# Second matrix product of a gated feed-forward block on one Trainium2 core: two of four hidden blocks as three float32r products

## The chip, the cores and the metric

The kernel runs on one core of one Trainium2 chip (trn2). The metric is the device time of one execution in microseconds, and lower is better. The engines are named as the profile names them: PE is TensorE, DVE is VectorE, ACT is ScalarE, POOL is GpSimd, and SP is the queue that issues most DMAs.

## The reference, cut to what matters

The input is 32 images of 128 channels and 56 x 56 pixels. A convolution of signs with batch norm is added to the input (phase 1 of the kernel, and the relu at the head of phase 2). Then each pixel is a token of 128 values, and the feed-forward part below is computed. Weights are float32, and so is the result.

```
weights = x @ wr + br                              # router, one number per token
sel     = the top k - 1 tokens of an image, k = 1568
h       = gelu(sel @ w1 + b1)                      # 128 -> 512
y       = (h @ w2 + b2) * weights[selected]        # 512 -> 128, the product that is changed
out     = scatter of y into zeros, + x
```

The kernel computes h and y for all tokens and multiplies y by a gate, which is zero for tokens that are not chosen.

## The kernel before, in words

An image is a [128 channels, 3136 tokens] tile, cut into 7 chunks of 448 tokens. Phase 1 (the first 500 us) centres the channels, takes signs, convolves and gathers the batch statistics. Phase 2 does everything else, image by image, and is the part that the change touches.

Phase 2 is a schedule that is written by hand. Every engine walks through the same 56 positions for an image (`POS`), 8 for a chunk, and does at each position what tables assign to it. At positions 0 to 3 of a chunk PE computes one hidden block each (`hidden`, three float16 products of 128x448 into one bank), and ACT applies the gelu and writes `hs` (L495, float32, a ring of two chunks with four blocks). At positions 4 to 7 PE multiplies the hidden blocks 0 to 3 of the chunk before by `w2_c` in float32 and sums them in one bank (`output`, L950). A block is so used 12 positions after it was computed, and ACT takes the sum after the fourth (L505).

The other work of phase 2 is put between these by the tables, in positions of an image. Those of interest here:

- `TRANSPOSE_AT`: PE transposes a chunk of the next image into one of two banks (L885), and DVE takes statistics of it (L647). The first four are at 1, 3, 4 and 5, the rest at 9, 10 and 11.
- Position 14: DVE turns the statistics into variances (L660 to L665). Position 15: POOL takes their power -0.5 (L426). Position 22: DVE `mean_over_std` (L670). Position 23: PE transposes mean and deviation (L904), DVE splits them in three (L676 to L679), and SP spreads them into rows by DMA. PE needs the rows at position 31 (L917).
- `NORM_AT`: PE spreads the statistics over the channels (L917, L920), DVE scales (L685) and centres (L694) the tokens, ACT and POOL write the high half `th` (L518) and the low half `tl` (L412), and DVE writes `base` (L702).
- `ROUTER_AT`: PE computes the router's products (L895), the last at position 27. DVE writes the row at 28 (L709), SP stores it and loads it back in another layout, and only then issues the load of the second half of the next `x` and `y`, which ACT waits for at position 37 (L511).
- `COUNT_AT`, eight rounds at positions 35, 39, 42, 46, 50, 53, 58 and 61 (58 and 61 are 2 and 5 of the next image): PE sums counts (L959), DVE chooses a threshold (L728, L733, L739) and counts again (L722). A round can't begin before the one before it has come back.
- Positions 66 to 69 (10 to 13): DVE and PE rank the ties, and DVE writes the gates (L767 to L775). SP spreads them by DMA, and PE needs them at position 19 (L930). DVE multiplies y by them (L781), and POOL adds `base` (L419).

Each engine takes its instructions in order, so one that waits holds back all that follow on its engine. The lines of the change are in `output` (PE), a new `hidden_high` on DVE and a new `hidden_low` on POOL.

## Time and profile before

| what | value |
|---|---|
| three runs | 2378.2, 2380.06, 2380.43 us; median 2380.06 |
| the profiled execution | 2379.78 us, its span 2377.8 us |
| PE, DVE, ACT, POOL busy in the span | 93%, 68%, 51%, 39% |
| mean granted clock of TensorE | 0.981 |
| from one power operation on POOL (one in each image) to the next, mean of 31 | 56.0 us, from 531.6 to 2267.8 us |

The page gives busy time of each engine for the whole span. Since the work of phase 2 repeats with the image, the more useful reading is one image in order of time: what each engine does at a position, and what it waits for there. The images alternate between some 58 and 55 us.

### The profile page before, as it was taken

How to read it: one execution, taken by the hardware profiler on the slowest of the kernel's cores; microseconds unless marked ns; L12 is line 12 of the kernel's file. 1: busy time of each engine (PE TensorE's matmuls, PEld its weight loads, DVE VectorE, ACT ScalarE, POOL GpSimd, SP SyncE). 2: the span in 40 equal slices, each digit the busy share in tenths (PEclk: the TensorE clock that was granted, in tenths of full speed). 3: DMA queues.
4: the chain of work that ended last, by engine and by line, in shares of the span. 5: the costliest groups of instructions: out<-in, count | busy, mean ns of one | idle time of the engine just before them, and what ended most of it. 6: DMA issues, size and time to landing. Idle time of an engine off the chain costs nothing. (4 is left out here: it accounts for less than half of the span.)

```text
span 2377.8 us, 38759 instructions
## 1 busy us (share of the span) xinstructions
PE 2202.0 (93%) x9739; PEld 1071.6 (45%) x9739; DVE 1622.5 (68%) x4887; ACT 1222.9 (51%) x2030; POOL 918.5 (39%) x714
## 2 busy tenths in 40 slices
PE   6999999966999999999999999998999999999997
PEld 3555555533444444444444444444444444444443
DVE  6777777755677766767676666666667676767764
ACT  4444444434555555555555555555555555555553
POOL 1000000024455544445445555454544454554433
PEclk9999999987999999999999999999999999999998
DMA  3444444431122222222222222222222222222201
GB/s 146 163 162 162 162 162 162 162 122 46 62 73 73 74 81 76 81 85 75 73 73 73 73 73 72 73 73 73 81 82 91 73 73 73 73 73 84 73 33 59
DMA packets 66710, 216.99 MB, mean 91 GB/s; under 512 B 28496, under 2 KB 33328, under 8 KB 62640
## 3 DMA queue, kind: packets, MB, share of 16 engines
q1 hardware_dynamic: 66464, 215.71, 25.1%
q14 instruction: 84, 0.69, 0.1%
q8 instruction: 18, 0.29, 0.1%
q10 hardware_dynamic: 144, 0.30, 0.0%
HBM read 136.70 MB, written 77.47 MB: 90 GB/s over the span
## 5 line engine op out<-in xcount | busy, mean ns | idle before, releaser
L950 PE MATMUL ps<-hs,w_c 128*128 128x448 f32 x1792 | 806.9, 564 | 0.8 <-ACT yo L505 0.6
L495 ACT ACTIVATE hs<-ps,b1c,undo 128x448 f32<-128x448 f32 x896 | 602.6, 718 | 136.6 <-PE ps L941 136.0
L412 POOL TENSOR_TENSOR tl<-tr,th 128x448 f16<-128x448 f32 x224 | 245.5, 1096 | 515.7 <-ACT th L518 393.9
L854 PE MATMUL ps<-yo,cwT 128*128 128x448 bf16 x2016 | 425.6, 356 | 0.0
L950 PEld LDWEIGHTS ps<-hs,w_c 128*128 128x128 f32 x1792 | 305.3, 192 | 191.7 <-issue 152.3
L505 ACT ACTIVATE yo<-ps,cols 128x448 f32<-128x448 f32 x224 | 141.9, 633 | 453.6 <-PE ps L950 453.6
L407 POOL TENSOR_TENSOR xb<-xb,zr 128x448 f32<-128x448 f32 x224 | 259.1, 1159 | 182.7 <-ACT zr L511 181.8
L419 POOL TENSOR_TENSOR yo<-yo,base 128x448 f32<-128x448 f32 x224 | 264.5, 1181 | 167.4 <-DVE yo L781 166.6
L939 PE MATMUL ps<-th,w_h 128*128 128x448 f16 x896 | 321.4, 359 | 0.0
L941 PE MATMUL ps<-th,w_l 128*128 128x448 f16 x896 | 319.3, 356 | 0.0
L940 PE MATMUL ps<-tl,w_h 128*128 128x448 f16 x896 | 319.2, 356 | 0.0
L854 PEld LDWEIGHTS ps<-yo,cwT 128*128 128x128 bf16 x2016 | 179.2, 98 | 196.2 <-issue 48.7
L476 ACT ACTIVATE y<-ps 128x448 f16<-128x448 f32 x224 | 121.9, 544 | 263.2 <-PE ps L854 263.2
L781 DVE TENSOR_TENSOR yo<-yo,ps 128x448 f32<-128x448 f32 x224 | 138.6, 619 | 152.4 <-PE ps L930 150.7
L647 DVE BATCH_NORM_STATS2 st<-ps 112x6 f32<-112x128 f32 x896 | 192.7, 282 | 62.9 <-PE ps L885 60.5
L511 ACT ACTIVATE zr<-y,bn_t,bn_s 128x448 f32<-128x448 f16 x224 | 168.8, 754 | 122.2 <-DMA y<-y_int 109.6
L685 DVE TENSOR_TENSOR ur<-xb,ps 128x448 f32<-128x448 f32 x224 | 138.5, 618 | 134.8 <-PE ps L917 76.5
L571 DVE BATCH_NORM_STATS2 base<-y 128x448 f16 (+1 forms) x224 | 140.5, 627 | 130.2 <-ACT y L476 130.2
L518 ACT ACTIVATE th<-tr 128x448 f16<-128x448 f32 x224 | 129.3, 577 | 139.8 <-DVE tr L694 127.6
L426 POOL TENSOR_TENSOR rm<-stw,kt 112x28 f32<-112x28 f32 x32 | 153.6, 4799 | 78.8 <-DVE stw L665 78.8
L885 PE MATMUL ps<-kt,xb 128*112 128x128 f32 x896 | 140.4, 281 | 41.7 <-DVE st L647 28.8
L403 POOL TENSOR_TENSOR sm<-sm,kt 128x1 f32<-128x1 f32 x1 | 0.6, 566 | 459.7 <-DVE sm L635 459.7
(131 smaller groups left out, 2709.7 us busy)
## 6 DMA issues: line engine op xcount, KB each, us to landing
xb<-x SPq DMA_DIRECT2D x31, 1568.0 KB, 7.6
xb<-x SPq DMA_DIRECT2D x33, 896.0 KB, 4.7
result<-yo SPq DMA_DIRECT2D x32, 896.0 KB, 4.4
y_int<-y SPq DMA_DIRECT2D x32, 784.0 KB, 3.7
xb<-x SPq DMA_DIRECT2D x33, 672.0 KB, 4.3
result<-yo SPq DMA_DIRECT2D x32, 672.0 KB, 3.4
y<-y_int SPq DMA_DIRECT2D x32, 448.0 KB, 5.3
y<-y_int SPq DMA_DIRECT2D x32, 336.0 KB, 4.8
```

The costliest lines, as they stand in the source:

```text
L407: nc.gpsimd.tensor_tensor(cut(xb[b], c), cut(xb[b], c), zr[(b + c) % 2][:, :], ALU.add).then_inc(x1_ready, 1)
L412: nc.gpsimd.tensor_tensor(cut(tl, c), tr[(b + c) % 2][:, :], cut(th, c), ALU.subtract).then_inc(tl_ready, 1)
L419: nc.gpsimd.tensor_tensor(cut(yo[b], c), cut(yo[b], c), cut(base[b], c), ALU.add).then_inc(out_ready, 1)
L426: nc.gpsimd.tensor_tensor(rm[:, 0, :], stw[:, 5, :], kt[0:TILE, K_MHALF:K_END], ALU.pow).then_inc(rstd_ready, 1)
L495: nc.scalar.activation(hs[(b + slot) % 2][:, j, :], ps[:, H_BANK + j, 0:T], ACT.Gelu_apprx_tanh, bias=b1c[:, j:j + 1], scale=undo[:, 1:2]) ...
L511: nc.scalar.activation(zr[(mb + c) % 2][:, :], cut(y16[mb], c), ACT.Relu, bias=bn_t[:, :], scale=bn_s[:, :]).then_inc(relu_ready, 1)
L647: last = V.bn_stats(st[:, c * TPG + i, :], ps[0:TILE, BC0 + c % 2, i * C:(i + 1) * C])
L854: last = M(bank, cwT[:, t, :], sg[b][:, c * ROWS + dy:c * ROWS + dy + ROWS, dx:dx + SIDE], start=t == 0, stop=t == TAPS - 1)
L939: M(bank, w1_h[:, blk], cut(th, c), start=True, stop=False)
L940: M(bank, w1_h[:, blk], cut(tl, c), start=False, stop=False)
L941: M(bank, w1_l[:, blk], cut(th, c), start=False, stop=True).then_inc(h_done, 1)
L950: last = M(bank, w2_c[:, j, :], hs[(b + c) % 2][:, j, :], start=first, stop=final)
```

## The change

Hidden blocks 0 and 1 of each chunk are no longer multiplied in float32. DVE casts `hs` to float32r (`hh`), POOL writes the rest `hl = hs - hh`, also float32r, and PE forms three float32r products for each block: `w2_h` x `hh`, `w2_h` x `hl`, `w2_l` x `hh`. The weights are split once, in phase 1. Blocks 2 and 3 stay as they were. The casts stand at positions 1 and 2 of a chunk on DVE, the subtractions at 2 and 3 on POOL.

```diff
+SPLIT = 2
...
+        w2_h = sb("w2_h", [C, SPLIT, C], f32r)
+        w2_l = sb("w2_l", [C, SPLIT, C], f32r)
...
+        hh = [sb(f"hh{b}", [C, SPLIT, T], f32r) for b in range(2)]
+        hl = [sb(f"hl{b}", [C, SPLIT, T], f32r) for b in range(2)]
...
+            def hidden_low(n, b, c, j):
+                pool.wait_ge(hh_ready, (n * NCH + c) * SPLIT + j + 1)
+                ring = (b + c) % 2
+                nc.gpsimd.tensor_tensor(hl[ring][:, j, :], hs[ring][:, j, :], hh[ring][:, j, :].bitcast(f32),
+                                        ALU.subtract).then_inc(hl_ready, 1)
...
+                    slot, j = divmod(pos, 2 * NB)
+                    if 2 <= j < 2 + SPLIT and has(n):
+                        hidden_low(n, b, slot, j - 2)
...
+            link(V.tensor_copy(w2_h[:, :, :], w2_c[:, 0:SPLIT, :]))
+            V.tensor_tensor(w2_l[:, :, :], w2_c[:, 0:SPLIT, :], w2_h[:, :, :].bitcast(f32), ALU.subtract)
...
+            def hidden_high(n, b, c, j):
+                dve.wait_ge(h_ready, (n * NCH + c) * NB + j + 1)
+                ring = (b + c) % 2
+                V.tensor_copy(hh[ring][:, j, :], hs[ring][:, j, :]).then_inc(hh_ready, 1)
...
+                    if 1 <= j < 1 + SPLIT and has(n):
+                        hidden_high(n, b, slot, j - 1)
...
-                last = M(bank, w2_c[:, j, :], hs[(b + c) % 2][:, j, :], start=first, stop=final)
+                ring = (b + c) % 2
+                if j < SPLIT:
+                    pe.wait_ge(hl_ready, g * SPLIT + j + 1)
+                    M(bank, w2_h[:, j, :], hh[ring][:, j, :], start=first, stop=False)
+                    M(bank, w2_h[:, j, :], hl[ring][:, j, :], start=False, stop=False)
+                    M(bank, w2_l[:, j, :], hh[ring][:, j, :], start=False, stop=False)
+                else:
+                    last = M(bank, w2_c[:, j, :], hs[ring][:, j, :], start=False, stop=final)
```

Three places show where the new instructions stand. The first is DVE between positions 23 and 34 of an image, from the end of the split of the statistics to the first count. Before:

```order
L702 SCALAR_TENSOR_TENSOR base<-tr,xb 128x448
L781 TENSOR_TENSOR yo<-yo,ps 128x448
L709 TENSOR_SCALAR wrow<-ps,undo,cols 7x448
L781 TENSOR_TENSOR yo<-yo,ps 128x448
L685 TENSOR_TENSOR ur<-xb,ps 128x448
L694 TENSOR_TENSOR tr<-ur,ps 128x448
L781 TENSOR_TENSOR yo<-yo,ps 128x448
L722 TENSOR_SCALAR junk,cnt_c<-wse,cand 128x392
```

And now (line numbers of the changed kernel; `hh<-hs` is the new cast):

```order
L720 SCALAR_TENSOR_TENSOR base<-tr,xb 128x448
L799 TENSOR_TENSOR yo<-yo,ps 128x448
L804 CAST hh<-hs 128x448 x2
L727 TENSOR_SCALAR wrow<-ps,undo,cols 7x448
L799 TENSOR_TENSOR yo<-yo,ps 128x448
L703 TENSOR_TENSOR ur<-xb,ps 128x448
L712 TENSOR_TENSOR tr<-ur,ps 128x448
L799 TENSOR_TENSOR yo<-yo,ps 128x448
L804 CAST hh<-hs 128x448
L740 TENSOR_SCALAR junk,cnt_c<-wse,cand 128x392
```

Two casts have come in ahead of the router's row, and one ahead of the first count.

The second is DVE at positions 40 to 45, between two rounds of the search. Before:

```order
L694 TENSOR_TENSOR tr<-ur,ps 128x448
L728 TENSOR_SCALAR reached,srch<-ps 128x15
L733 TENSOR_SCALAR srch<-srch,steps 128x1
L739 TENSOR_SCALAR srch<-srch,candc 128x1
L702 SCALAR_TENSOR_TENSOR base<-tr,xb 128x448
L722 TENSOR_SCALAR junk,cnt_c<-wse,srch 128x392
```

And now:

```order
L712 TENSOR_TENSOR tr<-ur,ps 128x448
L804 CAST hh<-hs 128x448
L746 TENSOR_SCALAR reached,srch<-ps 128x15
L751 TENSOR_SCALAR srch<-srch,steps 128x1
L757 TENSOR_SCALAR srch<-srch,candc 128x1
L804 CAST hh<-hs 128x448
L720 SCALAR_TENSOR_TENSOR base<-tr,xb 128x448
L740 TENSOR_SCALAR junk,cnt_c<-wse,srch 128x392
```

One cast stands ahead of the choice and one ahead of the next count. The rounds at 50 and 58 have the same pair around them.

The third is POOL from position 15 to 24. Before:

```order
L426 TENSOR_TENSOR rm<-stw,kt 112x28
L412 TENSOR_TENSOR tl<-tr,th 128x448
L407 TENSOR_TENSOR xb<-xb,zr 128x448
L419 TENSOR_TENSOR yo<-yo,base 128x448
L412 TENSOR_TENSOR tl<-tr,th 128x448
L407 TENSOR_TENSOR xb<-xb,zr 128x448
```

And now (`hl<-hs,hh` is the new subtraction):

```order
L439 TENSOR_TENSOR rm<-stw,kt 112x28
L419 TENSOR_TENSOR tl<-tr,th 128x448
L425 TENSOR_TENSOR hl<-hs,hh 128x448
L414 TENSOR_TENSOR xb<-xb,zr 128x448
L425 TENSOR_TENSOR hl<-hs,hh 128x448
L432 TENSOR_TENSOR yo<-yo,base 128x448
L419 TENSOR_TENSOR tl<-tr,th 128x448
L414 TENSOR_TENSOR xb<-xb,zr 128x448
```

Two subtractions have come in ahead of the second `tl`, which the router's last product needs.

## Rows read from the trace of the kernel before

**Rows 1.** The page: busy time of the engines, and two of its costliest groups.
```profile
PE 2202.0 (93%) x9739; PEld 1071.6 (45%) x9739; DVE 1622.5 (68%) x4887; ACT 1222.9 (51%) x2030; POOL 918.5 (39%) x714
...
L950 PE MATMUL ps<-hs,w_c 128*128 128x448 f32 x1792 | 806.9, 564 | 0.8 <-ACT yo L505 0.6
...
L511 ACT ACTIVATE zr<-y,bn_t,bn_s 128x448 f32<-128x448 f16 x224 | 168.8, 754 | 122.2 <-DMA y<-y_int 109.6
```

**Rows 2.** Busy time by stretch (length, engines, clock, DMA share, GB/s): an image, two parts.
```profile
1020.57:1078.37 57.80, 53.05 (x230) 24.88 (x228) 39.18 (x131) 31.04 (x50) 28.70 (x22) 1.00 0.21 75
...
1099.20:1124.50 25.30, 24.41 (x101) 11.37 (x101) 20.62 (x76) 13.16 (x22) 10.99 (x10) 1.00 0.32 124
1066.50:1078.40 11.90, 11.79 (x60) 6.51 (x61) 10.22 (x48) 5.86 (x10) 3.80 (x4) 1.00 0.29 109
```

**Rows 3.** Timeline of PE (start, length, engine, line, tiles): prices of products.
```profile
252.58 0.53 PE L844 MATMUL ps<-xh,centre_r 128*128 128x448 f32 x1
252.95 0.37 PE L845 MATMUL ps<-xl,centre_r 128*128 128x448 f32 x1
...
254.73 0.53 PE L844 MATMUL ps<-xh,centre_r 128*128 128x448 f32 x1
...
1089.78 0.35 PE L895 MATMUL ps<-th,wsel_h 128*128 128x448 f16 x1
1089.97 0.35 PE L895 MATMUL ps<-tl,wsel_h 128*128 128x448 f16 x1
...
1100.00 2.49 PE L950 MATMUL ps<-hs,w_c 128*128 128x448 f32 x6
1102.43 0.36 PE L930 MATMUL ps<-rows,ones_b 3*128 3x448 bf16 x1
```

**Rows 4.** Groups by line over the whole span: the cast nearest to the new one.
```profile
L547 DVE CAST xh<-xb 128x448 fp32r<-128x448 f32 x224 | 84.7, 378 | 7.2 <-PE ps L845 6.8 <-DVE cand L622 0.4
```

**Rows 5.** Timeline, POOL and DVE, 1078 to 1088 us: both engines on SBUF at once.
```profile
1078.37 4.80 POOL L426 TENSOR_TENSOR rm<-stw,kt 112x28 f32<-112x28 f32 x1 [2.48 <-DVE stw L665]
...
1084.13 1.14 POOL L407 TENSOR_TENSOR xb<-xb,zr 128x448 f32<-128x448 f32 x1
...
1086.31 1.04 POOL L412 TENSOR_TENSOR tl<-tr,th 128x448 f16<-128x448 f32 x1
...
1079.62 0.63 DVE L702 SCALAR_TENSOR_TENSOR base<-tr,xb 128x448 f32<-128x448 f32 x1
...
1084.72 0.59 DVE L670 SCALAR_TENSOR_TENSOR rm<-stw,rm 112x28 f32<-112x28 f32 x1
```

**Rows 6.** Timeline, 1105 to 1123 us: ACT, PE and DVE between rounds of the search.
```profile
1105.48 0.76 ACT L511 ACTIVATE zr<-y,bn_t,bn_s 128x448 f32<-128x448 f16 x1 [5.97 <-DMA y<-y_int]
...
1107.32 0.71 ACT L495 ACTIVATE hs<-ps,b1c,undo 128x448 f32<-128x448 f32 x1
...
1109.66 0.17 PE L959 MATMUL ps<-cand_sel,cnt_c 128*128 128x15 f16 x1
...
1122.64 0.62 PE L885 MATMUL ps<-kt,xb 128*112 128x128 f32 x4
...
1106.24 0.17 DVE L728 TENSOR_SCALAR_CACHE_REDUCE reached<-ps 128x15 f32<-128x15 f32 x1
...
1107.86 0.61 DVE L722 TENSOR_SCALAR_CACHE_REDUCE junk<-wse,srch 128x392 bf16<-128x392 f32 x1
```

**Rows 7.** Timeline, 1075 to 1100 us: PE and DVE where a DMA or a round ends a wait.
```profile
1081.34 0.34 PE L930 MATMUL ps<-rows,ones_b 3*128 3x448 bf16 x1 [0.28 <-DMA rows<-mks]
...
1095.11 0.36 PE L917 MATMUL ps<-rows,ones_b 3*128 3x448 bf16 x1 [1.10 <-DMA rows<-rms]
...
1099.90 0.18 PE L959 MATMUL ps<-cand_sel,cnt_c 128*128 128x15 f16 x1 [1.21 <-DVE junk L722]
...
1075.02 0.25 DVE L767 TENSOR_SCALAR mk<-ps,srch 98x32 f32<-98x32 f32 x1 [0.90 <-PE ps L972]
...
1090.55 0.73 DVE L709 TENSOR_SCALAR wrow<-ps,undo,cols 7x448 f32<-7x448 f32 x1 [0.50 <-PE ps L895]
```

More of the change, by code:

```diff
@@ L251, in block_kernel @@
         h_ready = sem("h_ready")
+        hh_ready = sem("hh_ready")
+        hl_ready = sem("hl_ready")
         y_done = sem("y_done")
@@ L781, in apply_gate @@
                 V.tensor_tensor(cut(yo[b], c), cut(yo[b], c), ps[:, BC1, 0:T], ALU.mult).then_inc(gated, 1)
+            def hidden_high(n, b, c, j):
+                dve.wait_ge(h_ready, (n * NCH + c) * NB + j + 1)
+                ring = (b + c) % 2
+                V.tensor_copy(hh[ring][:, j, :], hs[ring][:, j, :]).then_inc(hh_ready, 1)
             def phase2(n, b):
                 for pos in range(POS):
+                    slot, j = divmod(pos, 2 * NB)
                     at = (n, b, pos)
```

## The prediction

> **What bounds the kernel now.** I read the page first, then the busy time of single images and stretches, then the timelines of the engines in one image. The page [rows 1] shows PE busy for 93% of the span, with the float32 product L950 as its largest group, and DVE at 68%. That alone says: make PE cheaper. It doesn't say where PE's time can be taken away. In one image [rows 2] PE is busy for 53.05 of 57.80 us, DVE for 39.18, ACT for 31.04 and POOL for 28.70. But DVE's load is uneven. In the stretch of the search (positions 35 to 61) DVE is busy for 20.62 of 25.30 us, and in the next one, up to the variance, for 10.22 of 11.90. Its free time lies elsewhere, mostly between positions 19 and 35.
>
> PE has short waits where something else ends last [rows 7]: 0.28 us for the gates' rows (position 19), 1.10 us for the rows of statistics (position 31), and 1.21 us for the first count (position 35). All three are ends of chains that start on DVE or pass it. What is put on DVE ahead of them comes out on PE in full.
>
> **PE's price.** Three float32 blocks in a row take from 1100.00 to 1102.43 us, 0.81 us each [rows 3]. Float16 products start 0.19 us apart. In phase 1 a group of nine bfloat16 and two float32r products repeats every 2.15 us (252.58 to 254.73); less 9 x 0.19 that leaves 0.44, or 0.22 for a float32r product. Three of them make 0.66, so a block gains 0.15 us. The ends: 0.19 each (as float16) gives 0.57 and a gain of 0.24; 0.37 each (the distance from the first float32r product to the second, with the weight load in it) gives 1.11 and a loss of 0.30. I take 0.15, since the period counts both and everything around them. An image has 14 such blocks. Two (positions 28, 29) lie before the wait at 31, whose end is set by a DMA: worth nothing. The other 12 would give 1.8 us an image.
>
> **DVE's price.** The cast has a twin in phase 1, 0.378 us [rows 4], with POOL idle. Here POOL works. When both use SBUF they wait for each other: L670, with 28 elements a row, takes 0.59 us and ends at 1085.31, just after POOL's L407 has ended at 1085.27 [rows 5]. So a cast may wait for up to one whole POOL operation, 1.14 us, and at least for nothing. I take 0.5, about half of one: the first cast releases POOL's subtraction of the same block, and the second comes while that runs. A cast then costs 0.88 us, between 0.38 and 1.52.
>
> The Trainium skill (SBUF — State Buffer, engine side) says that VectorE in a two-port mode or with two SBUF inputs and GpSimd take a shared port pair as an exclusive lock for the whole instruction. It speaks against this change. L670 and L407 agree; the long power operation doesn't, see the rivals.
>
> **The sum, for one image.**
> 1. *Search, positions 35 to 61.* Six casts (41, 42, 49, 50, 57, 58) add 5.3 us to DVE's 20.62, which makes 25.9 in a stretch of 25.30: +0.6. PE's own saving there (eight blocks, 1.2 us) isn't seen, for DVE ends last. To this comes a new wait. The cast at 41 needs `hs` of position 40, and ACT has that only after the relu at 37, which waited 5.97 us for a DMA [rows 6]: ACT starts the gelu at 1107.32 and ends at 1108.03, while DVE had come to its choice at 1106.24. That is 1.8 us of waiting, with the choice, the candidate and the next count (1107.86) queued behind, and PE waits for that count at 1109.66. ACT's wait for that DMA is 109.6 us over 30 cases on the page's group (3.7 us on average, estimated from its total), so I take half of the 1.8: +0.9. Together +1.5 us. Bounds: -1.2 (all hidden, PE's saving whole) and +3.
> 2. *To the gates and the variance, positions 5 to 14.* Two casts (9, 10) add 1.8 us to 10.22 in 11.90 us. DVE's own wait of 0.90 us before the gates (1075.02) takes some of it, and the rest delays the gates, hence the DMA, hence PE at position 19, which waits for it already: +1.0. Bounds: 0 and +1.8. POOL's power operation begins that much later too, and so do the statistics.
> 3. *19 to 23.* Two blocks (20, 21) at 0.15: -0.3. Bounds -0.5 and +0.6. The casts at 17 and 18 fall into DVE's idle time; without it they would cost 0.8.
> 4. *23 to 35.* Two casts (25, 26) come between the statistics' split and the router's row, 1.8 us against DVE's wait of 0.50 us there (1090.55). The row's store and reload carry that to the first count, for which PE waits: +1.2. Bounds: 0 and +1.8. The casts at 33 and 34 come ahead of or with the wait for that reload: nothing, or 0.4 if it lands early.
>
> POOL gets 14 subtractions of about 1.14 us, 16 us an image on top of 28.70 in 57.80: 78% busy, not a bound on average. It is tightest behind the power operation. The `tl` that the router's last product needs ended at 1087.35 [rows 5] and moves by two subtractions to 1089.6; PE starts that product at 1089.78 [rows 3]. I cost it at nothing; if those 0.2 us are gone it is some 0.5 us an image. The products themselves come 10 positions after their subtraction, with POOL's lag well inside. Splitting the weights in phase 1 is two short operations in DVE's gaps: nothing.
>
> The sum is 1.5 + 1.0 - 0.3 + 1.2 = **+3.4 us an image**, with 32 images 109 us. Against the profiled execution of 2379.78 us (0.3 us below the median of the runs) that is **2488 us**, 4.6% slower. What a measurement of this kernel can tell from no change is about 0.2%, or 5 us.
>
> **The rivals.**
> - *PE's saving comes through.* DVE idles for 18.6 us an image, and 14 casts need 5.3 without port waits. If the port waits are short and ACT is early, casts slip into gaps and PE pays nothing. For it: PE is 93% busy, and most of DVE's idle time is waiting for PE. Against it: the two stretches where DVE is at 82% and 86%, and the search, in which DVE must answer PE each round. All of it gives 12 x 0.15 x 32 = 58 us, 2322; half of it 2351. It decides where DVE's additions in the search stay below its idle 4.7 us there with PE's 1.2 taken off, that is below 3.5 us or 0.58 a cast. Chance 0.22.
> - *Gains and waits cancel* within 5 us: 0.04.
> - *Every wait is met in full.* Items at their upper ends, 3 + 1.8 - 0.3 + 1.8 = 6.3 us an image: 2581. For it: casts and subtractions release each other, so collisions are systematic. Against it: delays of one chain partly cover those of the next. Chance 0.12.
> - *The power operation locks the casts out.* POOL's L426 takes 4.80 us in each image, and the casts at 17 and 18 come while it runs. Waiting for its end would delay the gate multiplication at 19 and PE behind it by some 2 us, 64 in all: 2552. Against it: a two-input operation of DVE ran inside it in 0.63 us, its usual time (1079.62) [rows 5]. Chance 0.03. This is what the Trainium skill's rule on that page (a lock held for the full instruction) would give when taken by the letter; the trace doesn't agree for this operation.
> - *The float32r triple isn't cheaper on PE.* At 0.37 us a product, 14 blocks lose 0.30 each: 134 us on PE alone, so 2514 even if nothing waits. The second float32r product of phase 1 came without such a delay. Chance 0.03.
>
> **How the numbers follow.** The forecast, slower through DVE, has 0.56; its own range is 2410 to 2560 (about +1 to +5.6 us an image). Slower in all: 0.56 + 0.12 + 0.03 + 0.03 = 0.74; same 0.04; faster 0.22. The range of 8 in 10 takes in the upper part of the faster cases and stops short of the full ones: 2330 to 2570.
>
> **What would show it.** In the changed profile L950's group must have half its records, and the triple must repeat every 0.6 to 0.7 us. If I am right, PE's busy time falls by some 50 to 70 us while its waits for DVE's count (L959) and for DMA rows grow by more; DVE shows casts with a mean well above 0.38 us and a spread up to 1.5; the time from one power operation to the next rises from 56.0 to about 59.4 us. It is wrong if casts take 0.38 to 0.45 us on average, if PE's waits for counts stay at about a microsecond an image, or if that period falls below 56.

## The result and the profile after

The changed kernel takes 2678.74 us (median of four runs, the lowest 2675.14), the kernel before in the same session 2380.00: a ratio of 1.1252, 95% interval [1.123, 1.1274], so 299 us slower. One of the four executions was in a slower state (2733.80 us); the ratio is of the other three. The forecast was slower by 109 us, to 2488. The direction was right, the size was not, and 2678.74 lies above the range of 2330 to 2570.

The page of the changed kernel: the busy times that answer to [rows 1], and groups by line (busy time, mean ns of one, idle time before, releaser).

```profile
PE 2268.8 (85%) x10187; PEld 1181.0 (44%) x10187; DVE 2059.6 (77%) x5337; ACT 1222.3 (46%) x2030; POOL 1480.1 (55%) x1162
...
L983 PE MATMUL ps<-hs,w_c 128*128 128x448 f32 x896 | 456.7, 619 | 0.0
...
L804 DVE CAST hh<-hs 128x448 fp32r<-128x448 f32 x448 | 289.6, 651 | 35.7 <-ACT hs L511 35.1
...
L720 DVE SCALAR_TENSOR_TENSOR base<-tr,xb 128x448 f32<-128x448 f32 x224 | 221.3, 988 | 0.1
```

The float32 group has half its records, as it must. But PE's busy time rose by 67 us instead of falling by 50 to 70. A float32 record now lasts 619 ns on average, where it lasted 564 [rows 1]. Sorted by the granted clock, the records at full clock are as before (567 ns, 560 before), and those at the lower level take 995 ns: there are 86 of these now, of 896, where there were 12 of 1792. So the mean rose because the granted clock fell. The casts' mean is 0.65 us. `base`, an old operation, rose from 735 ns (its group before the change) to 988 ns.

The groups of small VectorE operations on the gates and the statistics (`mean_over_std`, then two operations of the gates), first before the change, then after:

```profile
L670 DVE SCALAR_TENSOR_TENSOR rm<-stw,rm 112x28 f32<-112x28 f32 x32 | 18.0, 563 | 4.9 <-POOL rm L426 4.9
L769 DVE TENSOR_TENSOR mk<-mk 98x32 f32<-98x32 f32 x32 | 14.8, 463 | 1.1
...
L770 DVE TENSOR_TENSOR mk<-mk 98x32 f32<-98x32 f32 x32 | 6.1, 192 | 1.1
```

```profile
L688 DVE SCALAR_TENSOR_TENSOR rm<-stw,rm 112x28 f32<-112x28 f32 x32 | 94.9, 2964 | 5.1 <-POOL rm L439 5.1
...
L787 DVE TENSOR_TENSOR mk<-mk 98x32 f32<-98x32 f32 x32 | 31.4, 982 | 1.1
L788 DVE TENSOR_TENSOR mk<-mk 98x32 f32<-98x32 f32 x32 | 31.1, 973 | 1.1
```

The third operation of the gates (L789) rose from 192 to 569 ns, and a cast in the split of the statistics (L696) from 416 to 754 ns.

The list of waits (engine, line, what it waited for: us in total, times, longest), before the change:

```profile
PEld ps L959 <- DVE junk L722: 58.2, 67, 1.8
...
PE ps L885 <- DVE st L647: 28.8, 25, 1.3
PE ps L959 <- DVE junk L722: 24.1, 24, 1.3
...
PE ps L930 <- DMA rows<-mks: 8.5, 11, 5.7
```

And after, PE's loads of weights (PEld) and PE:

```profile
PEld ps L992 <- DVE junk L740: 141.6, 131, 3.9
...
PE ps L911 <- DVE st L665: 92.4, 43, 2.4
...
PE ps L992 <- DVE junk L740: 70.6, 76, 3.5
...
PE ps L956 <- DMA rows<-mks: 70.1, 32, 5.7
```

PE now waits for VectorE's counts, for its statistics, and for the DMA behind the gates.

Timeline of PE at the start of a search, the triple (start, length, engine, line, tiles):

```profile
1192.18 0.47 PE L979 MATMUL ps<-hh,w_h 128*128 128x448 f32 x1
1192.49 0.36 PE L980 MATMUL ps<-hl,w_h 128*128 128x448 f32 x1
1192.68 0.37 PE L981 MATMUL ps<-hh,w_l 128*128 128x448 f32 x1
1192.89 0.36 PE L979 MATMUL ps<-hh,w_h 128*128 128x448 f32 x1
1193.09 0.36 PE L980 MATMUL ps<-hl,w_h 128*128 128x448 f32 x1
1193.29 0.36 PE L981 MATMUL ps<-hh,w_l 128*128 128x448 f32 x1
1193.49 0.91 PE L983 MATMUL ps<-hs,w_c 128*128 128x448 f32 x2
```

From the second product on, the products start 0.20 us apart, and a triple repeats in 0.60 (1192.89 to 1193.49), against 0.81 for a float32 block [rows 3]. The gain is 0.2 us a block.

**One image in stages.** For each of these runs I took the starts of five VectorE operations from the timelines between 900 and 2000 us: V, the variance (L683); S, the first cast of the statistics' split (L694); K, the first count of the search; T, the ties (L770); G, the gates (L785). The line numbers are those of the changed kernel. Mean us from one to the next:

| run | image | V to S | S to K | K to T (search) | T to G | G to V |
|---|---|---|---|---|---|---|
| before | 56.93 | 9.22 | 11.67 | 26.61 | 6.49 | 2.94 |
| after | 67.09 | 10.97 | 12.26 | 31.20 | 7.80 | 4.77 |
| triple_only | 56.55 | 8.99 | 11.98 | 25.95 | 6.46 | 3.17 |
| casts_only | 62.21 | 8.98 | 12.04 | 31.09 | 6.95 | 3.13 |
| lows_only | 59.36 | 10.55 | 12.12 | 26.40 | 6.18 | 4.10 |
| casts_on_act | 60.70 | 10.28 | 12.45 | 26.78 | 6.64 | 4.54 |
| search_on_act | 61.55 | 11.01 | 12.25 | 26.58 | 7.22 | 4.50 |
| rest_on_act | 66.18 | 9.56 | 12.69 | 31.89 | 7.39 | 4.60 |
| casts_later | 65.53 | 10.85 | 12.61 | 30.16 | 6.53 | 5.01 |
| lows_late | 67.14 | 10.07 | 13.36 | 31.23 | 7.82 | 4.67 |
| search_split_dve | 61.30 | 9.10 | 11.92 | 30.28 | 6.97 | 2.99 |
| search_split_act | 56.36 | 9.25 | 11.74 | 26.04 | 6.32 | 3.00 |
| early_split_act | 60.22 | 9.67 | 12.64 | 26.81 | 6.43 | 4.61 |
| before_earlier | 56.75 | 7.90 | 12.96 | 26.55 | 6.37 | 2.97 |

Of the 10.2 us that an image grows, 4.6 arise in the search, 3.1 from the ties to the variance, 2.3 from there to the first count. Over the whole program the power operations of POOL tell the same: the first starts at 532.7, the 32nd at 2562.5, 65.5 us each instead of 56.0 (+9.5; with 32 images 304 us).

From one variance to the next in the same window, PE idles for 11.27 us an image where it idled for 3.72, and is busy for 55.82 us where it was for 53.21. So three quarters of the growth are waits of PE. The rest is PE taking longer for its work.

### The profile page after: what moved, and what is told of

Same layout as the page of the kernel before. It is cut to its first block and busy times, and to the rows that moved or that the text cites. A ratio compares the mean times of both kernels' runs of the same rounds, so it can differ in the third digit from the quotient of the medians.

```text
span 2676.7 us, 41662 instructions
## 1 busy us (share of the span) xinstructions
PE 2268.8 (85%) x10187; PEld 1181.0 (44%) x10187; DVE 2059.6 (77%) x5337; ACT 1222.3 (46%) x2030; POOL 1480.1 (55%) x1162
## 5 line engine op out<-in xcount | busy, mean ns | idle before, releaser
L425 POOL TENSOR_TENSOR hl<-hs,hh 128x448 fp32r<-128x448 f32 x448 | 546.6, 1230 | 70.4 <-DVE hh L804 70.4
L983 PE MATMUL ps<-hs,w_c 128*128 128x448 f32 x896 | 456.7, 619 | 0.0
L965 PE MATMUL ps<-th,w_h 128*128 128x448 f16 x896 | 333.1, 372 | 0.0
L966 PE MATMUL ps<-tl,w_h 128*128 128x448 f16 x896 | 331.8, 370 | 0.0
L967 PE MATMUL ps<-th,w_l 128*128 128x448 f16 x896 | 330.5, 369 | 0.0
L432 POOL TENSOR_TENSOR yo<-yo,base 128x448 f32<-128x448 f32 x224 | 284.4, 1270 | 70.2 <-DVE yo L799 69.3
L804 DVE CAST hh<-hs 128x448 fp32r<-128x448 f32 x448 | 289.6, 651 | 35.7 <-ACT hs L511 35.1
L703 DVE TENSOR_TENSOR ur<-xb,ps 128x448 f32<-128x448 f32 x224 | 138.7, 619 | 180.2 <-PE ps L943 95.7
L911 PE MATMUL ps<-kt,xb 128*112 128x128 f32 x896 | 147.6, 291 | 115.6 <-DVE st L665 92.4
L720 DVE SCALAR_TENSOR_TENSOR base<-tr,xb 128x448 f32<-128x448 f32 x224 | 221.3, 988 | 0.1
```

The source lines that it names most:

```text
L425: nc.gpsimd.tensor_tensor(hl[ring][:, j, :], hs[ring][:, j, :], hh[ring][:, j, :].bitcast(f32), ALU.subtract).then_inc(hl_ready, 1)
L432: nc.gpsimd.tensor_tensor(cut(yo[b], c), cut(yo[b], c), cut(base[b], c), ALU.add).then_inc(out_ready, 1)
L720: V.scalar_tensor_tensor(cut(base[b], c), tr[ring][:, :], 1.0 / T_SCALE, cut(xb[b], c), ALU.mult, ALU.add).then_inc(base_ready, 1)
L804: V.tensor_copy(hh[ring][:, j, :], hs[ring][:, j, :]).then_inc(hh_ready, 1)
L965: M(bank, w1_h[:, blk], cut(th, c), start=True, stop=False)
L966: M(bank, w1_h[:, blk], cut(tl, c), start=False, stop=False)
```

## Experiments

Each edit is against the changed kernel unless it says otherwise, and each ratio is to the kernel before, with its 95% interval.

### Four parts, one at a time

**triple_only**: neither casts nor subtractions. ACT writes `hh` as float32r, and the middle product reads `hh` again, so the low halves of h are left out.

```diff
-nc.scalar.activation(hs[(b + slot) % 2][:, j, :], ps[:, H_BANK + j, 0:T],
+dest = hh if j < SPLIT else hs
+nc.scalar.activation(dest[(b + slot) % 2][:, j, :], ps[:, H_BANK + j, 0:T],
...
-hidden_high(n, b, slot, j - 1)
...
-hidden_low(n, b, slot, j - 2)
...
-pe.wait_ge(hl_ready, g * SPLIT + j + 1)
...
-M(bank, w2_h[:, j, :], hl[ring][:, j, :], start=False, stop=False)
+M(bank, w2_h[:, j, :], hh[ring][:, j, :], start=False, stop=False)
```

> TensorE's part of the change alone: ScalarE writes hidden blocks 0 and 1 as float32r itself, and TensorE forms the three float32r products from it (the block's low half is left out: the second product reads the high half again). No casts, no subtractions. The trace of the changed kernel has a triple at 0.60 us against 0.81 for a float32 block, so both theories expect faster than before: 12 blocks x 0.2 us x 32 images = 77 us, 2300 to 2325 us. If it comes out above 2380, the products themselves cost the time (rival: the triple isn't cheaper in place).

2364.15 us, 0.9929 [0.991, 0.9949]. PE's saving is real and small. 14 blocks at 0.2 us would be 90 us in all, and 16 come through; the expected 2300 to 2325 was too low. The clock took part of it: the lower level was granted for 161 us of this run, against 94 before the change. The search gets shorter by 0.7 us an image, an image by 0.4.

**casts_only**: the casts stay, the subtractions and `hl` go as above (low halves left out), and PE waits for the casts.

> VectorE's casts and the triple, without GpSimd's subtractions (the low half is left out: the second product reads the high half again). Theory A (the casts lengthen VectorE's own chains, wherever the port is free): most of the 299 us stays, 2550 to 2650. Theory B (VectorE and GpSimd wait for each other at SBUF, above all VectorE's old two-input operations behind runs of GpSimd operations): casts cost their 0.38 us with GpSimd as busy as before, so 2340 to 2450, and the small operation on mean and deviation takes about 0.6 us again instead of 3.9.

2522.99 us, 1.0585 [1.0556, 1.0614]: 159 us over triple_only, and between the ranges of the two theories. The operation on mean and deviation took 0.68 us, as theory B had it, but the casts cost far more than their 0.38 us each. All of it stands in the search (25.95 to 31.09) and in T to G.

**lows_only**: ACT writes `hh`, POOL forms `hl = hh - hh` (low halves left out).

> GpSimd's subtractions and the triple, without VectorE's casts (ScalarE writes the high half as float32r; the subtraction reads that tile twice, so the low half is zero, with the same shapes and positions). Theory A (casts): about as fast as without them, 2310 to 2360. Theory B (collisions): slow although VectorE has no new instruction, 2420 to 2560, with the operation on mean and deviation at some 3 to 4 us and base's at 0.9 us or more.

2447.14 us, 1.0276 [1.0256, 1.0297], in the range of theory B: 83 us over triple_only, most of it outside the search (V to S +1.6, G to V +0.9). The subtraction took 0.97 us here, reading one tile twice, where it takes 1.23 in the changed kernel, so this cost is a low one.

**load_only**: casts, subtractions and PE's waits for them as in the change, but PE multiplies in float32.

```diff
-M(bank, w2_h[:, j, :], hh[ring][:, j, :], start=first, stop=False)
-M(bank, w2_h[:, j, :], hl[ring][:, j, :], start=False, stop=False)
-M(bank, w2_l[:, j, :], hh[ring][:, j, :], start=False, stop=False)
+M(bank, w2_c[:, j, :], hs[ring][:, j, :], start=first, stop=False)
```

> Casts and subtractions as in the change, TensorE waits for them, but multiplies all four blocks in float32 as before. If TensorE's saving is lost behind the waits anyway (both theories), this is within 30 us of the changed kernel's 2679, so 2660 to 2710. If the changed products help to throttle TensorE's clock (fewer and shorter products in the gaps), this one holds a higher granted clock than the changed kernel's 0.938 and isn't slower.

2674.39 us, 1.1234 [1.1215, 1.1253]. With the load on VectorE and POOL in place, the cheaper product is worth nothing that can be measured. Two readings remain. PE may not be the bound any more; or the cheaper product lowers the clock and loses by it what it saves. The expectation named the sign of the second, a granted clock above 0.938 in a kernel that isn't slower, and it came: 0.950 to 0.958 in the four runs. The runs don't decide between the two. Against triple_only the casts add 159, the subtractions 83, both together 315, so 73 us belong to the pair.

### Where the casts cost

**casts_on_act**: every cast is an ACT copy behind the next block's gelu.

```diff
+if 1 <= j < 1 + SPLIT and has(n):
+    act.wait_ge(h_ready, g * NB + j)
+    nc.scalar.activation(hh[ring][:, j - 1, :], hs[ring][:, j - 1, :],
+                         ACT.Copy).then_inc(hh_ready, 1)
...
-if 1 <= j < 1 + SPLIT and has(n):
-    hidden_high(n, b, slot, j - 1)
```

> The change, with the 14 casts of an image on ScalarE instead of VectorE (same positions, copies behind the gelu), subtractions where they were. The 2x2 of casts and subtractions (2364, 2447, 2523, 2679) says that taking VectorE's casts away gives back 232 us with subtractions in place. So 2440 to 2490 if what counts is VectorE. If it is the cast's latency or the traffic on SBUF from whichever engine, it stays above 2600.

2483.98 us, 1.0458 [1.0443, 1.0474]: 195 us back. A copy takes ACT 0.57 us, and the search is at 26.78 us, nearly the 26.61 of before.

**search_on_act** and **rest_on_act**: only the casts of chunks 5, 6 and 0 (six an image, in the search) on ACT, or only the other eight. Of search_on_act, VectorE's line and ACT's (rest_on_act has `in` and `not in` the other way round):

```diff
+SEARCH = (5, 6, 0)
...
-if 1 <= j < 1 + SPLIT and has(n):
+if 1 <= j < 1 + SPLIT and slot not in SEARCH and has(n):
...
+if 1 <= j < 1 + SPLIT and slot in SEARCH and has(n):
```

> The change, with the six casts of an image that fall into the search (chunks 5, 6 and 0, positions 41, 42, 49, 50, 57 and 58) moved to ACT, each right behind the gelu of the block after; the other eight casts stay on VectorE. All is computed as in the change. Theory (the main cost of the change is the casts that stand inside the rounds of the search on VectorE): the stretch from the first count to the ties falls from 31.2 us an image back to 26.5 to 27.5, the stretches from the gates to the statistics stay as in the change, and the time falls by most of what moving all the casts gave (195 us), to 2520-2570. Rival (casts cost about the same wherever they stand, so six of fourteen bring 6/14 of 195 = 84 us): 2590-2610, with the rest spread over the other stretches.

> The complement: the eight casts of an image outside the search on ACT (chunks 1 to 4), the six in the search on VectorE. All is computed as in the change. Theory: the stretch from the first count to the ties stays at 30.5 to 31.5 us, little is gained elsewhere, and the time is 2620-2665. Rival (each cast costs the same): 8/14 of 195 = 111 us less, 2555-2580. A second rival: the subtractions of POOL collide with two-input operations of VectorE whatever engine casts, so that even the stretches outside the search don't shorten and the time stays at 2665-2680.

2511.95 us, 1.0551 [1.0524, 1.0578], a little below the expected 2520 to 2570, and 2658.76 us, 1.1176 [1.1147, 1.1205], as expected. Six casts in the search are worth 167 us, 0.87 each; eight outside are worth 20, 0.08 each. The sum, 187, is nearly the 195 of moving all. This tells the two theories apart: a cast on VectorE has no fixed price of its own, its place sets it.

How it comes about is seen on VectorE between two rounds of the search in the changed kernel:

```profile
1205.03 0.62 DVE L712 TENSOR_TENSOR tr<-ur,ps 128x448 f32<-128x448 f32 x1
1205.57 0.97 DVE L804 CAST hh<-hs 128x448 fp32r<-128x448 f32 x1
1206.46 0.16 DVE L746 TENSOR_SCALAR_CACHE_REDUCE reached<-ps 128x15 f32<-128x15 f32 x1
...
1207.10 0.58 DVE L804 CAST hh<-hs 128x448 fp32r<-128x448 f32 x1
1207.60 0.61 DVE L740 TENSOR_SCALAR_CACHE_REDUCE junk<-wse,srch 128x392 bf16<-128x392 f32 x1
...
1208.67 1.57 DVE L720 SCALAR_TENSOR_TENSOR base<-tr,xb 128x448 f32<-128x448 f32 x1
```

And PE at the ends of the same rounds:

```profile
1202.62 0.18 PE L992 MATMUL ps<-cand_sel,cnt_c 128*128 128x15 f16 x1 [1.20 <-DVE junk L740]
1205.60 0.17 PE L992 MATMUL ps<-cand_sel,cnt_c 128*128 128x15 f16 x1
1208.28 0.18 PE L992 MATMUL ps<-cand_sel,cnt_c 128*128 128x15 f16 x1 [0.22 <-DVE junk L740]
```

PE had the sum of the round ready at 1205.77 (1205.60 and 0.17), but VectorE was in a cast and came to the choice only at 1206.46. Another cast stands ahead of the next count. Both lie in series with the round.

The same stretch by load (busy time of the engines, then clock, DMA share, GB/s; of 27 us VectorE is busy for 25.74, where [rows 2] had 20.62 of 25.30):

```profile
1192.00:1219.00 27.00, 22.75 (x104) 12.37 (x105) 25.74 (x74) 13.80 (x23) 21.24 (x18) 0.99 0.24 90
```

From K to T, in the mean of an image, the records of VectorE's seven casts (the seventh is that of position 34, which follows the first count) sum to 5.5 us, 0.78 each. Those of its four `base` rose from 3.0 to 5.1, and its idle time fell only from 5.72 to 3.76 (neighbouring records overlap by some tenths, so these don't add up to 4.6 exactly). `base` doesn't explain the search by itself. In search_on_act its records sum to 4.6 us and the search takes 26.58; in casts_only they sum to 3.3 and the search takes 31.09.

Nor does VectorE's load. In casts_only the seven casts sum to 3.8 us, VectorE's idle time even rose, to 6.8, and the search was as long as in the change. There PE's idle time rose from 1.9 us (triple_only) to 4.5, and its busy time from 24.1 to 26.6, at a granted clock of 0.89 from K to T. So each engine waited for the other, and about half of the growth in that run is PE taking longer for the same products. In the changed kernel PE's idle time there is 5.7 us and its clock 0.93.

**casts_later**: casts at positions 3 and 4 of a chunk, subtractions at 5 and 6.

```diff
-if 1 <= j < 1 + SPLIT and has(n):
-    hidden_high(n, b, slot, j - 1)
+if 3 <= j < 3 + SPLIT and has(n):
+    hidden_high(n, b, slot, j - 3)
...
-if 2 <= j < 2 + SPLIT and has(n):
-    hidden_low(n, b, slot, j - 2)
+if 5 <= j < 5 + SPLIT and has(n):
+    hidden_low(n, b, slot, j - 5)
```

> The change, with the casts at positions 3 and 4 of a chunk instead of 1 and 2, and the subtractions at 5 and 6 instead of 2 and 3. All is computed as in the change. Step 1 of the prediction had half a cost of 0.9 us an image from a cast that stands in the queue before ACT has written its input. Theory (that wait is small, VectorE waits 35 us in all for ACT in the change, and VectorE's load decides): nothing much moves, 2640-2690. Rival (waiting for ACT's block, with a choice and a count queued behind, is a main cost): the wait goes, and the time falls by 50 us or more, below 2630.

2627.56 us, 1.1028 [1.1004, 1.1052]: 51 us less, which is the rival's side by a narrow margin. Casts that wait for ACT's block fell from 35.1 to 0.2 us. But of the 1.6 us that an image is shorter, the search gave only 1.0; T to G gave 1.3, and V to K and G to V together took some 0.5 back (the stages' means cover slightly different images). L688 also fell, from 2964 to 601 ns, and the subtractions had moved as well, so ACT's lateness isn't cleanly separated from the new neighbours.

**split_one**: `SPLIT = 1`, half of everything.

> Half the dose: SPLIT = 1, one of the four blocks in three float32r products, so seven casts and seven subtractions an image (one cast in each of the chunks, at position 1 of it). Theory (VectorE is past its limit in the search only with the second cast of a chunk, and costs grow faster than the dose): 2480-2520, less than half of the change's 299 us. Rival (costs in proportion): 2380 + 150 = 2530 or more, as when every cast and subtraction has a price of its own.

2503.76 us, 1.0506 [1.0483, 1.0529]. The first block costs 123 us, the second 175: more than in proportion, as expected, though not by much.

### Where the subtractions cost

Timeline of VectorE and POOL behind the power operation in the changed kernel:

```profile
1174.40 4.00 DVE L688 SCALAR_TENSOR_TENSOR rm<-stw,rm 112x28 f32<-112x28 f32 x1
```

```profile
1172.97 1.04 POOL L419 TENSOR_TENSOR tl<-tr,th 128x448 f16<-128x448 f32 x1
1173.97 1.13 POOL L425 TENSOR_TENSOR hl<-hs,hh 128x448 fp32r<-128x448 f32 x1
1175.06 1.13 POOL L414 TENSOR_TENSOR xb<-xb,zr 128x448 f32<-128x448 f32 x1
1176.15 1.12 POOL L425 TENSOR_TENSOR hl<-hs,hh 128x448 fp32r<-128x448 f32 x1
1177.24 1.12 POOL L432 TENSOR_TENSOR yo<-yo,base 128x448 f32<-128x448 f32 x1
1178.32 1.03 POOL L419 TENSOR_TENSOR tl<-tr,th 128x448 f16<-128x448 f32 x1
```

An operation on 28 elements a row starts at 1174.40, while POOL's first subtraction runs, and ends at 1178.40. That is just after POOL's `yo` (1177.24 and 1.12), the fourth operation of POOL that ends in the meantime. PE stands behind it:

```profile
1178.46 0.36 PE L930 MATMUL ps<-kt,rm 112*28 112x112 f32 x2 [1.83 <-DVE rm L688]
1187.12 0.36 PE L943 MATMUL ps<-rows,ones_b 3*128 3x448 bf16 x1 [1.86 <-DMA rows<-rms]
```

**lows_late**: the third chunk's subtractions from positions 18 and 19 to 24 and 25.

```diff
-if 2 <= j < 2 + SPLIT and has(n):
+if 2 <= j < 2 + SPLIT and slot != 2 and has(n):
     hidden_low(n, b, slot, j - 2)
+if pos in (24, 25) and has(n):
+    hidden_low(n, b, 2, pos - 24)
```

> The change, with the two subtractions of the third chunk moved on GpSimd from positions 18 and 19 to 24 and 25, so that the run behind the power operation is as it was before the change. Theory B (VectorE's small two-input operation on mean and deviation is held through a longer run of GpSimd operations): that operation falls from 3.9 to about 0.6 us, the way from the power operation to the rows of statistics shortens by 1.7 us an image, and the time falls by 40 to 70 us to 2610 to 2640. Theory A (only the casts on VectorE matter): no change, 2670 to 2685.

2691.06 us, 1.133 [1.1311, 1.1349]: both expectations fell, for it is slower than the change. L688 did fall to 632 ns, and V to S to 10.07 us. But S to K rose by 1.1 us, and PE's wait for the rows of statistics from 61.5 to 87.0 us in all. The collision had moved to a cast in the split, whose mean rose from 754 to 1963 ns:

```profile
L698 DVE CAST rms<-rrest 28x224 bf16<-28x224 f32 x32 | 62.8, 1963 | 1.1
```

**casts_on_act_lows_late**: that move together with all casts on ACT.

> The change with all casts on ACT, and the subtractions of the third chunk of an image moved from positions 18 and 19 to 24 and 25 on POOL. All is computed. Theory (what counts there is POOL's load between the power operation and the second low half for the router, not one place of it): the statistics are split earlier but the low half for the router or the split's own operations meet the moved subtractions, so the time stays within 15 us of 2484. Rival (the run of POOL operations right behind the power operation is the cost): 2400-2450.

2499.32 us, 1.0502 [1.0476, 1.0528], 15 us above casts_on_act, at the edge of the expected 15. The rival's 2400 to 2450 fell: the run of POOL operations behind the power operation isn't the cost by itself. The same cast of the split has a mean of 1341 ns here, against 845 in casts_on_act.

**search_split_act**, **search_split_dve** and **early_split_act** split only some chunks: 4, 5 and 6, whose subtractions stand in or just ahead of the search, with the casts on ACT or on VectorE, and 0 to 3 (early_split_act) with the casts on ACT. The same condition stands ahead of the subtraction, and a block that is not split stays in float32.

```diff
+SPLIT_CHUNKS = (4, 5, 6)
...
-if 1 <= j < 1 + SPLIT and has(n):
+if 1 <= j < 1 + SPLIT and slot in SPLIT_CHUNKS and has(n):
...
-if j < SPLIT:
+if j < SPLIT and c in SPLIT_CHUNKS:
```

> Only the chunks 4, 5 and 6 of an image are split (their products stand at positions 44, 45, 52, 53, 60 and 61, inside the search), with the casts on ACT; chunks 0 to 3 stay in float32. All is computed. POOL's subtractions then stand at 34, 35, 42, 43, 50 and 51, none of them between the ties and the split of the statistics. Theory (casts cost only on VectorE inside the search, and subtractions only between the ties and the router's row): both costs are gone and PE's saving in the search is left, first count to ties 25.9 to 26.6 us, all other stretches as before: 2360-2385. Rival (a subtraction costs wherever it stands, some 104 us for 14 in the run with all casts on ACT): 6/14 of it, 2420-2430.

> The same three chunks split, casts on VectorE as in the change (33, 34, 41, 42, 49 and 50, four of them inside the search). All is computed. Theory: the search stretch alone grows, by some two thirds of the change's 4.6 us, to 29 to 30 us, the stretches from ties to the split of the statistics stay at their values before; 2460-2510. Rival (the costs of the change need both, casts and the long runs on POOL near the statistics): under 2440.

> The complement: chunks 0 to 3 split, casts on ACT, chunks 4 to 6 in float32. All is computed. Subtractions at 2, 3, 10, 11, 18, 19, 26 and 27. Theory (what is left once the casts are off VectorE, 104 us, comes from these subtractions): the gates-to-variance and variance-to-split stretches grow as in the run with all casts on ACT (4.5 and 10.3 us), the search is as before, 2450-2490. Rival (cost per subtraction): 8/14 of 104, 2430-2445.

| run | us | ratio, interval |
|---|---|---|
| search_split_act | 2364.41 | 0.9945 [0.9931, 0.9958] |
| search_split_dve | 2496.82 | 1.0506 [1.0474, 1.0539] |
| early_split_act | 2476.64 | 1.0426 [1.0409, 1.0444] |

All three came as the theory had them. With six subtractions an image in or ahead of the search some of PE's saving is left: search_split_act computes everything and is faster than the change and than the kernel before, by 13 us against the latter. Six blocks at 0.2 us would be 38 us, so the six subtractions and ACT's copies cost at most the other 25. Six casts on VectorE instead of ACT cost 132 us. The eight early blocks cost 99 us. ACT's eight copies are in that number too, and no run takes them out of it. But lows_only had no copies at all and grew in the same stretches. Half of the 3.3 us an image are two small operations (G to V, 4.61 against 3.00 in search_split_act). In early_split_act:

```profile
L795 DVE TENSOR_TENSOR mk<-mk 98x32 f32<-98x32 f32 x32 | 31.9, 998 | 1.1
L796 DVE TENSOR_TENSOR mk<-mk,wk 98x32 f32<-98x32 f32 x32 | 31.1, 973 | 1.1
L704 DVE TENSOR_TENSOR rms<-rrest,rms 28x224 bf16<-28x224 f32 x32 | 27.7, 866 | 1.1
L703 DVE CAST rms<-rrest 28x224 bf16<-28x224 f32 x32 | 25.9, 808 | 1.1
```

and in search_split_act:

```profile
L703 DVE CAST rms<-rrest 28x224 bf16<-28x224 f32 x32 | 12.3, 384 | 1.1
L704 DVE TENSOR_TENSOR rms<-rrest,rms 28x224 bf16<-28x224 f32 x32 | 12.1, 379 | 1.1
...
L795 DVE TENSOR_TENSOR mk<-mk 98x32 f32<-98x32 f32 x32 | 6.2, 192 | 1.1
L796 DVE TENSOR_TENSOR mk<-mk,wk 98x32 f32<-98x32 f32 x32 | 6.1, 192 | 1.1
```

The two instructions of the gates (L795, L796) take 0.8 us longer each. In one image of early_split_act the first of them ends just after POOL's two subtractions of positions 10 and 11 (1103.42 and 2.22 give 1105.64; 1104.64 and 1.05 give 1105.69):

```profile
1103.42 2.22 POOL L426 TENSOR_TENSOR hl<-hs,hh 128x448 fp32r<-128x448 f32 x2
...
1104.64 1.05 DVE L795 TENSOR_TENSOR mk<-mk 98x32 f32<-98x32 f32 x1
```

The two operations of the split (L703, L704) are 0.9 us longer together, which is what S to K grew by. The rest (0.4 in V to S, 0.2 in the search) isn't laid on single instructions.

**search_split3_act** and **search_split4_act**: `SPLIT = 3` and `4` in search_split_act.

> As the kernel that split chunks 4, 5 and 6 with casts on ACT (2364.4 us, 0.9945 of before), but three of the four blocks of those chunks in three float32r products. All is computed. Six blocks gave 13 of the 38 us that 0.2 us a block would be. If the saving comes through at that rate: 6 us more, 2352-2362. Rival (POOL with three subtractions a chunk between its other work, or ACT with three casts, delays a low half or a gelu that PE needs): 2368-2400.

> The same with all four blocks of chunks 4, 5 and 6. All is computed. At the same rate 2344-2360. Rival (POOL's load, four subtractions of 1.2 us in about seven us beside two to three other operations, makes a low half late): 2375-2450.

2388.66 us, 1.0032 [1.0011, 1.0053], and 2417.81 us, 1.0169 [1.015, 1.0189]. Both lie in the ranges of their rivals: the gain doesn't go on. With four blocks POOL is busy for 1368.1 us instead of 1142.1, and L695 (`mean_over_std` again) rises from 532 to 1938 ns although no subtraction was put near it. POOL waited less ahead of the power operation (43.7 us in all instead of 78.4), so its queue seems to come late out of the search and to meet it there; this wasn't tested by itself.

### Clock and slack

**filler**: two float32 products, whose results are not used, ahead of the output at position 60, where PE waits.

```diff
+if j == 0 and c == NCH - 1:
+    pe.wait_ge(h_ready, g * NB + 3)
+    for _ in range(2):
+        M(bank, w2_c[:, 2, :], hs[ring][:, 2, :], start=True, stop=True)
```

> The change, with two needless float32 products more in each image on TensorE, in front of the first output product at position 60 (they write the output bank, which the real product then starts anew). Theory C (TensorE's clock falls to its lower level after the wait for statistics at position 61, and that costs): the products fill part of a wait of 2.2 us, the clock holds, the stretch at half clock behind it (4 records in 3.0 us instead of 1.7) is gone, and the kernel isn't slower: 2630 to 2685, with a granted clock above 0.938. Rival: the clock is only a symptom, and the products cost their time where TensorE isn't waiting: 2690 to 2730.

2668.95 us, 1.1234 [1.1216, 1.1251], within the expected time, but the granted clock was 0.932 and not above 0.938. The 10 us against the change don't hold: the ratios to the kernel before in the same session are 1.1234 and 1.1252, with overlapping intervals. In the changed kernel the clock falls after waits of PE. In one such place PE waits for 2.13 us until 1149.48, the lower level is granted from 1150.0 us, and the next wait follows:

```profile
1153.11 1.07 PE L911 MATMUL ps<-kt,xb 128*112 128x128 f32 x4 [1.94 <-DVE st L665]
1153.98 0.22 PE L992 MATMUL ps<-cand_sel,cnt_c 128*128 128x15 f16 x1
1154.05 3.13 PE L983 MATMUL ps<-hs,w_c 128*128 128x448 f32 x4
```

```profile
1153.00:1158.00 5.00, 4.89 (x15) 2.47 (x16) 3.32 (x17) 0.63 (x1) 0.00 (x0) 0.61 0.66 257
```

Two float32 blocks take 3.13 us there, twice 1.57, where one takes 0.81 at 2.4 GHz [rows 3]: this is the lower level, 1.2 GHz. From 900 to 2000 us the mean granted clock is 0.992 before and 0.929 after.

How many of the 299 us are the clock's own stays open; filler was the only attempt, and it didn't raise it. The traces give an upper bound, as an estimate. The lower level was granted for 94 us before and 334 after, and PE was busy for 53 and 271 us of that time. At half speed half of this busy time is lost: 26 us before, 136 after, 109 more. PE would have waited for part of these in any case.

**before_earlier** is against the kernel before: the statistics' split and the router's last product one and two positions earlier (`STAT_AT` 23 to 22, `ROUTER_AT` 27 to 25).

> The kernel before, with two entries of its tables moved: the statistics' rows one position earlier (22 instead of 23) and the router's last product two positions earlier (25 instead of 27). In the profile of the kernel before TensorE waits 1.1 us for the first chain's DMA and 1.2 us for the second's count in an image. If these waits are what they seem, both shorten by about a microsecond, 2 us x 32: 2320 to 2360. If something else comes late in their place (the gates, the load of y), within 10 us of 2380.

2372.18 us, 0.9989 [0.998, 0.9998], not the expected 2320 to 2360 but within 10 us of 2380, the other case that was named. V to S gave 1.3 us, S to K took 1.3 back: the chain before the first count isn't held by those positions.

## Why the prediction was wrong in size

- **PE's price held, its worth was overrated.** 0.22 a product was forecast, 0.20 measured, the block gains 0.2 instead of 0.15. But the rival by which all of it comes through (2322) is out of reach even with no cost at all: triple_only stands at 2364.15.
- **Step 1 (+1.5 an image, bounds -1.2 and +3) failed, and is the largest error: +4.6 measured.** Its price of a cast, 0.88 us, was somewhat high (seven from K to T take 0.78 each, so six take 4.7 us, not 5.3). What failed is the subtraction after it: "that makes 25.9 in a stretch of 25.30: +0.6". It set the casts against 4.7 us of VectorE's idle time as if that could be filled. It is idle while a round goes through PE, and a cast that starts in it ends beyond it. Of the 5.72 us of idle time only 2 were used, and in casts_only none. The runs give 0.87 us for a cast in the search and 0.08 for one outside. The second part of the step, waiting for ACT's block, was of the right kind (35.1 us in all before casts_later took it to 0.2).
- **A term was missing: the clock.** The sum took PE's work at full clock and had its busy time fall. The granted clock fell from 0.981 to 0.938, and PE's busy time rose. The bound worked out above is 109 us of the 299.
- **A term was missing: the old small operations.** The port wait was charged to the new casts alone, 0.5 us each; their mean, 0.65 instead of 0.88, was below that. POOL went from 918.5 to 1480.1 us of work, and old operations of VectorE were held: L688, L787 to L789 and L696. `base` was too, by 0.25 us each (735 to 988 ns), but search_on_act shows a short search with a long `base`, so no run shows that this one costs time.
- **Step 2 (+1.0, bounds 0 and +1.8) measured +3.1** (T to V, 9.43 to 12.57). It counted two casts. What it left out are L787 to L789, 1.7 us longer together. The way that it named, late gates, then the DMA, then PE at position 19, was right: PE's wait for the gates' rows grew from 8.5 to 70.1 us in all.
- **Steps 3 and 4 (+0.9 together) measured +2.3** (V to K, 20.89 to 23.23). "POOL gets 14 subtractions of about 1.14 us" and "I cost it at nothing" failed. They looked at what waits for POOL's results and not at the VectorE operations that are held while POOL works. L688, 0.6 us before and 3.0 after, and L696 are the cases. With casts_on_act 104 us of cost remain, for the subtractions and ACT's copies together.
- **The rival "the power operation locks the casts out" didn't come.** The 62 casts that ran wholly beside it took 0.55 us on average and none over 0.80, the 31 `base` beside it 0.62 each. The operation behind it was held, by others.
- **The rival "every wait in full" (2581)** was nearest, and still 98 us short, since it shared the missing terms.
- Of the signs named beforehand, half the records, 0.6 to 0.7 for a triple, a cast's mean above 0.38 and PE's growing waits came. PE's busy time and the period (65.5, not 59.4) told that the account was short.
- One row was misread, without effect on the sum: the product at 1089.78 [rows 3] is the one with `th`, and the one with `tl` starts at 1089.97.

## What to carry to other kernels

Idle time inside a ping-pong between two engines is the other engine's turn and not free: price what is put there at no less than its full length (here 0.87 us for a cast of 0.78), and only what is put outside by the idle time. When work is given to an engine that shares SBUF with another, look for the other's small operations that stand on the critical path, not only for those that wait for its result. Look at the granted clock as well: more waits of TensorE came with a lower clock here, and with it longer products. A cheaper product pays where its preparation can be placed so that it holds up neither: here that was three of seven chunks, with casts on ScalarE, for 0.55%.

## What was not expected of the hardware

A VectorE operation that was held didn't always get in after one operation of POOL: L688 lasted through the ends of up to four, with a median of 3904 ns over 32 (lows_only: mean 3193). Other operations of VectorE, `base` at 1208.67 (1.57 us) or the cast at 1205.57 (0.97), were held for less than one. The Trainium skill (SBUF — State Buffer, SBUF: two separate sides) has the loser wait for the whole instruction of the winner; the trace agrees that it waits, and shows waits longer than one instruction. In early_split_act the same operation (L695 there) meets the same run of POOL operations at the same point, 1.45 us after the power operation at 1115.01 as against 1.40 at 1174.40 in the changed kernel. It takes 0.70 us there and ends after the first of them. So the run of operations doesn't decide by itself, nor does the moment of the start, and why it loses four times in succession stays open.

POOL's two-input subtraction takes 0.93 us in the median when both inputs are the same tile (lows_only) and 1.14 when they differ; with the casts on ScalarE it is 1.13. And six small transfers in a row (`rows<-rms`) keep SP's queue for 4.84 us in lows_late, from 1111.94, 0.8 each, with the store of the router's row behind them at 1116.98.
